# The order of TensorE's work follows one of six rules in each stretch of two key tiles of an attention kernel

## The reference

```python
q, k, v = heads(norm(x) @ Wq.T + bq), heads(ctx @ Wk.T + bk), heads(ctx @ Wv.T + bv)
scores = einsum('bhqd,bhkd->bhqk', q, k) / sqrt(8)
attn = softmax(scores)            # layer 2: sigmoid(scores)
x = x + einsum('bhqk,bhkd->bhqd', attn, v) @ Wo.T + bo
...
w, idx = top_k(softmax(norm(x) @ router), 2)
x = x + sum(w[e] * expert_e(norm(x)) for e in idx)   # layer 1 does this part twice
```

## Time and profile before

| | |
|---|---|
| median of 3 runs | 4254.57 us |
| profiled execution, its own time | 4269.69 us |
| its span, first to last instruction | 4266.5 us |
| time outside the span | 3.2 us |
| opening, to the first score of the attention | 0 to 169.8 us |
| 32 phases | 169.8 to 4154.6 us |
| experts of the last block | 4154.6 to 4266.5 us |
| mean granted TensorE clock, whole span | 0.937 of full speed |

### The profile page before, as it was taken

The page is one execution under the profiler, slowest core; times in us unless marked ns, Lnnn a source line. Parts: engine busy times, 40 slices in busy tenths (PEclk is TensorE's granted clock), DMA queues, the critical chain, the costliest instruction groups (busy, mean ns, idle before and its releaser), DMA issues.

```text
span 4266.5 us, 71761 instructions
## 1 busy us (share of the span) xinstructions
PE 3834.3 (90%) x27716; PEld 1070.9 (25%) x27716; DVE 2936.6 (69%) x6154; ACT 3630.2 (85%) x4076; POOL 905.1 (21%) x1004
## 2 busy tenths in 40 slices
PE   8899998999989999898899899899999899899984
PEld 2122222222122222232221233241112322222213
DVE  6888997887978879776490233229499577789903
ACT  3699998898988989878799887789999889889980
POOL 3000003221032220444400433430000210121114
PEclk7699999998999999988999999899999989999996
DMA  6211102110011111222100223230000210110003
GB/s 147 75 29 35 26 24 58 38 30 19 13 51 44 52 38 31 58 55 66 38 17 16 78 74 105 67 91 16 16 15 18 81 37 15 33 42 26 12 10 88
DMA packets 155518, 189.86 MB, mean 45 GB/s; under 512 B 34728, under 2 KB 110512, under 8 KB 155088
## 3 DMA queue, kind: packets, MB, share of 16 engines
q1 hardware_dynamic: 129648, 113.27, 10.3%
q0 software_dynamic: 24800, 71.53, 5.8%
q10 hardware_dynamic: 720, 0.40, 0.0%
HBM read 146.66 MB, written 39.40 MB: 44 GB/s over the span
## 4 chain that ended last, share of the span: by engine, by line
PE 50%; ACT 18%; DVE 15%; issue 8%; another core or an unknown queue 3%; POOL 2%; DMA 0%; POOLq 0%; ACTq 0%; DVEq 0%
PE av L1446 22%; ACT prob L1612 15%; DVE mpart L1706 11%; PE scores L1431 11%; PE side L1467 7%; DVE above L1710 2%; PE side L1562 2%; PE scores L1551 2%; PE scores L1458 1%; ACT above L1621 1%; PE side L1551 1%; PE scores L1589 1%; PE scores L1585 1%; PE side L1431 0%
## 5 line engine op out<-in xcount | busy, mean ns | idle before, releaser
L1612 ACT ACTIVATE prob<-scores 128x1024 f32<-128x1024 f32 (+1 forms) x3103 | 2980.6, 1033 | 275.4 <-PE scores L1431 145.3
L1706 DVE TENSOR_REDUCE mpart<-side 128x1 f32<-128x512 f32 (+1 forms) x3648 | 2189.4, 656 | 360.1 <-PE side L1467 295.0
L1446 PE MATMUL av<-prob,VA 128*9 128x512 f32 x6400 | 862.7, 612 | 0.5
L1446 PE MATMUL av<-prob,VB 128*9 128x512 f32 x6400 | 862.5, 612 | 0.5 <-ACT prob L1612 0.2
L1431 PE MATMUL scores<-QP,KA 32*128 32x512 f16 x3080 | 599.9, 396 | 104.2 <-ACT prob L1612 49.5
L1467 PE MATMUL side<-KA,QP 32*128 32x512 f16 (+1 forms) x2144 | 594.8, 396 | 80.2 <-DVE mpart L1706 47.4
L1431 PE MATMUL scores<-QP,KB 32*128 32x512 f16 x3068 | 598.9, 392 | 48.1 <-ACT prob L1612 23.6
L1467 PE MATMUL side<-KB,QP 32*128 32x512 f16 (+1 forms) x2176 | 568.1, 385 | 71.8 <-DVE mpart L1706 43.2
L1710 DVE CUSTOM_DVE_ANT_0 above<-side,above 128x512 f32<-128x512 f32 x672 | 440.4, 686 | 99.6 <-PE side L1467 63.8
L1621 ACT ACTIVATE above<-scores 128x1024 f32<-128x1024 f32 x336 | 345.2, 1027 | 94.5 <-DVE mpart L1710 41.8
L1431 PEld LDWEIGHTS scores<-QP,KA 32*128 32x128 f16 x3080 | 143.4, 91 | 859.9 <-ACT prob L1612 669.5
(11 more groups left out here) (234 smaller groups left out, 2576.1 us busy)
## 6 DMA issues: line engine op xcount, KB each, us to landing
KA<-kstacks SPq DMA_DIRECT2D x384, 48.0 KB
KB<-kstacks SPq DMA_DIRECT2D x384, 48.0 KB
kstacks<-hi SPq DMA_DIRECT2D x100, 128.0 KB
ctxc<-in_ctxT SPq DMA_DIRECT2D x36, 256.0 KB
slots<-xslot SPq DMA_DIRECT2D x30, 256.0 KB
yslot<-slots SPq DMA_DIRECT2D x30, 256.0 KB
gates<-in_mask SPq DMA_DIRECT2D x16, 400.2 KB, 3.4
kstacks<-lo SPq DMA_DIRECT2D x50, 128.0 KB
```

The lines of the kernel that those rows point to most:

```text
L1446: last = pe.matmul(AV[ROWS * h:ROWS * h + VC, cols], v, at, start=kt == 0, stop=kt == LAST)
L1612: act.activation(dst, src, ACT.Exp if softmax(l) else ACT.Sigmoid, scale=SCALE).then_inc(sem["exp"], 1)
L1706: dve.tensor_reduce(part, bank, AX.X, ALU.max).then_inc(sem["red"], 1)
```

## The change

`steps` no longer uses one set of rules. For the plan of all eight blocks it goes through a string `RULE_OF` of 808 digits. Each digit names one of six entries of `RULES` and holds until 4 more scores are taken (`STRETCH`, two key tiles; 808 x 4 = 3232). After that `RULES[0]` is used again. Entry 0 is the set of before. Each of the others changes one or two numbers: entry 1 has `av_late` 0.1 instead of 0.4; entry 2 has `starve` 0 instead of 0.3; entry 3 has `dif_first` False; entry 4 has `starve` 0.6 and `av_late` 0.8; entry 5 has `back_late` 0.1 instead of 0.4. The digits were found by a search over the planner. They are: 299 times 0, 223 times 1, 221 times 3, 33 times 4, 17 times 5 and 15 times 2. The added condition in `choose` matters only where `split` is True, and it is False in all six entries, so the values' matmuls stay one step. No step is added or removed.

```diff
--- before.py
+++ after.py
@@ -969,7 +969,7 @@
             r = self.ready(av)
             if r is None or r > self.t:
                 av = None
-            elif av.key[2] == 0 and not self.rules.split:
+            elif av.key[2] == 0 and (not self.rules.split or av.key[1] in (0, LAST)):
                 av = Step("PE", "av", av.key[:2] + (1,), "whole")
         if self.scores:
             p, kt, half = self.scores[0]
@@ -1104,6 +1104,11 @@
             self.t = max(t, self.t + 1e-4)
 
     def steps(self):
+        if self.units == list(range(8)):
+            for i in range(len(RULE_OF)):
+                self.rules = RULES[int(RULE_OF[i], 16)]
+                self.advance(max(0, len(self.scores) - STRETCH))
+            self.rules = RULES[0]
         self.advance(-1)
         assert not self.scores and not self.avs and self.p is None and not any(q for x in self.heads.values() for q in x)
         return self.out
@@ -1116,7 +1121,26 @@
 STARVE, SLIP = 0.3, 0.03
 FFN_FROM, FFN_TO, KV_FROM, KV_TO = 12, [130, 130, 110, 110, 45, 85, 170], 24, [0, 280, 240, 200]
 Rules = namedtuple("Rules", "split starve av_late back_late dve_low slip dif_first")
-RULES = [Rules(False, 0.3, 0.4, 0.4, 0.5, 0.03, True)]
+RULES = [
+    Rules(split=False, starve=0.3, av_late=0.4, back_late=0.4, dve_low=0.5, slip=0.03, dif_first=True),
+    Rules(split=False, starve=0.3, av_late=0.1, back_late=0.4, dve_low=0.5, slip=0.03, dif_first=True),
+    Rules(split=False, starve=0.0, av_late=0.4, back_late=0.4, dve_low=0.5, slip=0.03, dif_first=True),
+    Rules(split=False, starve=0.3, av_late=0.4, back_late=0.4, dve_low=0.5, slip=0.03, dif_first=False),
+    Rules(split=False, starve=0.6, av_late=0.8, back_late=0.4, dve_low=0.5, slip=0.03, dif_first=True),
+    Rules(split=False, starve=0.3, av_late=0.4, back_late=0.1, dve_low=0.5, slip=0.03, dif_first=True),
+]
+STRETCH = 4
+RULE_OF = (
+    "3133333333100311333010310033333333333333331043041001031133333333333311014010103333333333333331103011"
+    "4031110001053330001120152403133003013003011121530033000313331101533333043110003333433333333333110111"
+    "1003331333100013334112113314013303130315033111151143300023110131003031233013130312113333201233330310"
+    "1300340311113333004401400200003010330343311103004343331100111111001000000000000011111111111100000010"
+    "0011111100000000000000000000000000000000010000000000000000000000000010000001000100000000000000000000"
+    "0010000001111110400040405044010000000000000000000000000401111400121120041111111110111101111111111111"
+    "1111110111010000000030333333333331341110033041303553533301520325051500441011000131033333333333333331"
+    "1111340033333333013013105320030100100133001030143303413114335330131331501130011000000011111111111111"
+    "11111110"
+)
 
 
 def attention_steps(units):
```

## The result

The changed kernel takes 4280.52 us (median of 9 runs, 4266.97 to 4286.54). The kernel before, run beside it, takes 4256.45 us (9 runs). The ratio is 1.0055, with a 95% interval of 1.0041 to 1.0068. The change is slower by 24 us, where 49 us less were forecast.

What follows compares the result with a forecast made beforehand. No engine was full; ACT's 437.4 us of idle time in the phases bounded the gain. Savings of 14 us (eight phases) and 35 (eighteen) made 49: 4254.6 - 49 = 4205.6, say 4206 us, range 4160 to 4262.

Steps and rivals of the forecast that it cites:

- The account: In the 32 phases: any gain must come out of ACT's 437.4 us of idle time.
- The eight phases: Phases with maxima and no experts, 40.0 us of ACT idle: 14 us saved, three quarters of 18.4.
- The eighteen: Phases with experts, routing or projections in the background, 383.7 us of ACT idle: 35 us saved, a fifth of 173.
- The second derivation: Check on the sum: a fifth of the 252.7 us of ACT's waits that TensorE ends, 50 us.
- Entry 3: Scores ahead of `dif` in 221 stretches: same ACT work, values start earlier; DVE's slack, 9.3 us a phase, absorbs later passes.
- Entry 1: Values wait for a score in 223 stretches: about 0.25 us won for ACT where it fires, against some 0.2 of TensorE's slack.
- What stays costs 0: Same steps, durations and awaited operands, no bank, buffer or DMA added; swaps in SP and GpSimd queues are free: 0.
- Rival C: Values held back idle TensorE and lower its clock, about 9 us a stretch: slower, about 4269 us; chance 0.05.
- Rivals A and B: A: saving in the plan only, about 4250 us, chance 0.12. B: overfitted order in expert phases, about 4275 us, 0.10.
- Switching: Weight loads on entering values steps, 0.26 us each: more switching costs at most 10 us; 49 saved if the count stays.
- The markers: Signs of being right: eight phases 1 to 3 us shorter each, six within 1 us, expert ones 2 us shorter in mean.
- The sign for being wrong altogether: In the eight clean phases: DVE's busy share going above 97% while ACT's idle time grows.

Runs made afterwards that it cites:

- e2: Changed kernel with only the digits 3 kept, all others 0 (entry 3 alone): 4327.73 us, 1.0134 of the kernel before.
- e1: Changed kernel with every digit 3 set to 0 (no entry 3): 4317.05 us, 1.0109 of the kernel before.
- e6: Changed kernel with only the digits 1 kept, all others 0 (entry 1 alone): 4140.23 us, 1.0146 of the kernel before.
- e13: The kernel of e6 again (entry 1 alone), in another group of runs: 4317.19 us, 1.0112 of the kernel before.
- e14: e13 with the same order and 65 additions of zero-weight matmuls shaped like values, after 2.4 planned us of 32-row work: 4302.36 us, 1.0077 of the kernel before.
- e4: Changed kernel with another digit string, one digit for 24 stretches, from a search counting tail time 1.4 fold: 4241.35 us, 0.9928 of the kernel before.
- e8: Changed kernel with another string, one digit for 24 stretches, from entries 0, 2, 4 and 5 alone: 4059.55 us, 0.9937 of the kernel before.
- e11: Changed kernel with another string, one digit for 8 stretches, all six entries, tail time counted 1.4 fold: 4231.69 us, 0.9915 of the kernel before.
- e12: Changed kernel with another string, one digit for 8 stretches, from entries 0, 2, 4 and 5 alone: 4229.90 us, 0.9906 of the kernel before.
- e15: e13's digits, but entry 1 counts as 0.4 once 2.2 us pass without values or other whole-array work: 4272.10 us, 1.0000 of the kernel before.
- e3: Changed kernel, same order, with extra 32-row matmuls in the tails, results thrown away: 4310.17 us, 1.0106 of the kernel before.
- e9: Changed kernel, same order, with extra whole-array matmuls in the tails, results thrown away: 4292.30 us, 1.0040 of the kernel before.
- e5: The changed kernel itself, run again in another group: 4110.07 us, 1.0067 of the kernel before.

## Why the prediction was wrong

- **The account.** Right: the change acted on ACT's idle time in the phases, and ACT's busy time stayed.
- **The size of the saving.** Both terms failed as they were formed. The eight phases, where I took 14 us off because nothing unplanned happens there, have 25 us more idle time of ACT (65.1 for 40.0). The eighteen, where I took 35 off, have 1 us less. That 54 us are gone at full clock outside tails, close to 49, is luck: my sum was by kind of phase and knew neither tails nor more half clock. The second derivation (a fifth of TensorE's waits) failed too. ACT's row for scores went from 154.3 up to 173.3 us. The first exponentials of phases hold 35 us of it for 14 before; all others wait 138 us for 140, in 219 cases for 321, so the small misfits became fewer and longer.
- **Entry 3.** This is the step that failed. It said that ACT has the same work either way and that DVE has 9.3 us of slack in each phase to take up the later passes. That counts work and not its order. The put-off `dif`s can't be made up in parallel: `above` is single, so each costs a turn of ACT and two of DVE in a row, and the next phase's scores wait for the last. DVE's slack did not help: it grew, from 74.5 to 920.9 - 800.10 = 120.8 us in the eight phases, as DVE waited (for maxima of the kind "both" 150.8 us for 60.4) while the chain ran late. ACT's idle time in tails is 66.5 us more. In e2, entry 3 alone, it is 72 us more (130.6 for 58.6) and the time 55 us longer. Of the changed kernel's loss no share can be given to entry 3, since without it (e1) the kernel is slower.
- **Entry 1.** The example in the earlier trace rows is right as far as it goes (0.25 us for ACT), but I priced a single choice and not a run of them. Alone it costs 1.1 to 1.5% (e6, e13); in e13 47 of the 56 us by which ACT's idle time in the phases rose are at half clock outside tails.
- **"What stays costs 0".** The key projections of the next layer were moved to where their context had not yet landed: TensorE waits 14.8 us for it in 6 cases, 4.09 us in the tail shown, and before it never did. I had given SP's queue nothing.
- **Rival C** named the clock, at 5%, and was half right. Its sign came, a mean clock below 0.93 (0.920). But I let it work through idle time, and a busy share doesn't tell: phase 16 keeps the full clock with TensorE busy for 86.51 of 95.40 us. What went ahead of the falls inside the eight phases was an interval of mostly 4 us and more without a values step. And of the 23.5 us in the table half clock outside tails holds 11. For the kernel before I took 319 us at half clock in the phases and 100 us of ACT's idle time in them; by its pieces it is 336 us, and 138.3 us outside tails alone. For a us at half clock I took 0.31 us from one window; e14 gives 0.17 to 0.45.
- **Rivals A and B** (misfit around stops) don't explain it. Both have their place in the eighteen phases, where ACT's idle time stayed; B's time of about 4275 us is near the result by luck. e4, e8, e11 and e12 are tuned to the same plan, in coarser steps, and are faster.
- **Switching.** The weight loads of values wait 417.2 us in 1611 cases for 412.3 in 1595: 5 us, so this term was rightly small.
- **The markers.** The six phases of the earlier trace rows changed by 3.0 us in sum (580.5 for 583.5), none by more than 1.7 us, where I gave 1. The eight of the earlier trace rows fell from 933.7 to 920.9 us, close to the forecast 14, but only because work left them. Phase 2 grew by 17.7 us with its tail, and phase 27 lost 12.8. The eighteen rose by 34 us, where I had them fall by 35. The sign for being wrong altogether was misplaced as well: ACT's idle time in the eight grew while DVE's busy share fell, from 92 to 87%.

Why would a search choose an order with such tails? The planner as written prices TensorE's steps alike at all times and knows no clock. The tails themselves it sees, so a search on its time alone may have traded them for shorter waits elsewhere. That is an argument from the source; no run shows what the search saw. On the chip the trade loses.

**What stays open.** Why entries 1 and 3 together lose less than either alone. The changed kernel's half clock outside the tails costs only 11 us more than before in the table, less than 0.45 x 89 = 40. Either the new pieces fall where ACT has enough queued to ride over them, or the idle time they would cost is booked under the tails; no run separates these. Nor did I measure what the late context chunks alone cost.

## What to carry to other kernels

When an order is rearranged by rules, look for what is put off rather than for what is won: work that ends in a serial chain (one buffer, two engines in turn) must not be left for the end of a phase, however much slack its engine shows on average. A planner that knows no clock can pick slow orders where it goes long without the engine's whole-array matmuls; a limit on that interval took entry 1 alone from 1.1% slower to no change (e15). A surcharge on the tails together with coarser digits took the same six rules from 0.5% slower to 0.9% faster (e11). And compare the idle time of the bounding engine, not the length of a phase. And price a rule by the longest run of its choices, not by one of them.

## What the runs showed of the hardware

- In the eight phases without experts, outside tails, TensorE's clock fell from 2.4 to 1.2 GHz although the engine was busy for 75 to 93% of the 3 us before (after, e1, e13). Most of these falls came in or just behind intervals of 4 to 7.8 us from one values step to the next, in which it ran 32-row matmuls. The kernel before has no such fall, with the longest interval at 4.3 us and with windows of about the same busy share (87 and 89%).
- Added matmuls differed in effect: of 32 rows they took half clock in the tails from 88 to 65 us (e3), of the whole array from 88 to 32 (e9).
- At half clock a score matmul took 0.60 us for 0.39, two values steps 3.60 us for 2.10. The cost to the kernel was 0.17 to 0.45 us for each us inside the phases (estimate from e13 and e14). In the tails, where a chain of ACT and DVE is in the way, taking 56 us of half clock out changed the time by nothing that could be measured (e9).
- The same kernel took 4082 us beside e5 to e8 and 4256 to 4273 us otherwise, 4.6% between 4082 and 4270, with mean clocks of 0.963 to 0.967 and 0.933 to 0.939. The chip's number is the same for e5 to e8 and e13 to e15. The changed kernel and entry 1 alone were slower than the kernel before at both levels.
